# Expert stage: TensorE reads a slot's weight address behind the gate/up block of the slot ahead

## The chip, the cores and the metric

One core of a Trainium2 chip. The metric is the device time of the kernel in microseconds (us). The engines of the core are TensorE (PE; its weight loads are PEld), VectorE (DVE), ScalarE (ACT), GpSimd (POOL) and SyncE (SP).
## The reference

Cross-attention on 64 x 64 tokens of width 256, then a mixture of eight experts with two experts for each token:

```python
x = x + xattn(layernorm(x), ctx_2048, ...)          # 16 heads; not touched by the change
h = layernorm(x)
probs = softmax(h @ gate_w.T); topw, sel = top_k(probs, 2)
combine = topw / sum(topw), put at the columns sel   # (T, E), T = 4096, E = 8
g, u = split(h @ w1[e].T)                            # w1: (8, 2*176, 256)
expert_out[e] = (silu(g) * u) @ w2[e].T              # w2: (8, 256, 176)
x = x + sum over e of combine[:, e] * expert_out[e]
```

## The kernel before

The first part, up to about 358 us, does the attention, the routing and the sorting: each token's normalised row is written twice to a table in HBM (sorted_rows), grouped by expert. A short plan then gives 72 slots of 128 rows each, and for every slot the first row and the offset of its expert's weights. All experts' weights lie in the on-chip memory (we_h and we_l, a high and a low part). The offsets are 72 whole numbers in slot_w, a view of the tile square.

The expert stage, 372 to 536 us, runs over the 72 slots in a software pipeline. In turn i, TensorE does four blocks, each for another slot:

- tr_hs(i), L1321: two transposes of the slot's rows (hs). They wait for the DMA that loads the rows.
- gate_up(i-1), L1328: six matmuls of 352 columns (L1110, L1111, L1112, twice each). They wait for h2_l_ready, which VectorE sets when it has made the low part of the transposed rows (L1068), behind ScalarE's high part (L703).
- tr_act(i-2), L1339 and L1340: two transposes of silu(g) * u. They wait for act_ready (ScalarE L709, VectorE L1075).
- down(i-3), L1342: six matmuls of 256 columns, with the same three lines. They wait for au_l_ready (ScalarE L714, VectorE L1081).

Behind them ScalarE copies the result (L721) and GpSimd scatters it to HBM (L528). A last stage of some 40 us loads these results, adds the two of each token and stores the output.

gate_up and down address the weights by a register. weights_of(m), L1324 to L1326, fills it: a load of one word of slot_w into a register of TensorE's sequencer (TENSOR_LOAD), with register work around it (FUSED_REGOPS in the trace, ISA in the program) and a check of the bounds. gate_up(i-1) and, two turns later, down(i-3) use the same register, kept in found[r].

The turns come in passes of RING = 12. The first pass is written out, five passes are a loop on each engine (Fori, L1397), and three last turns are written out again. found lives in one pass: in the turns r = 0 and r = 1 the down block's slot belongs to the pass before, and its address is read anew, just ahead of down. In the views tiles are named by the memory that they share: late is hs, xt_h and xt_l are the transposed rows, probs is the activation, at_h and at_l the transposed activation, and bank is the PSUM memory.

Of the kernel before, what the change touches and what calls it, by code (L numbers as in the profile page):

```python
# [36 lines left out]
NSLOT = 72  # L37
RING = 12
# [47 lines left out]
def build_in(nc, stack, x, ctx_t, w_proj, w_out, w_exp, w_gate, bias, norm_q, norm_k, out,  # L86
# [1018 lines left out]
    def _(pe):  # L1105
# [3 lines left out]
        def three(dst, a_h, a_l, b_h, b_l, start, stop):  # L1109
            pe.matmul(dst, a_h, b_h, start=start, stop=False)  # L1110
            pe.matmul(dst, a_h, b_l, start=False, stop=False)  # L1111
            return pe.matmul(dst, a_l, b_h, start=False, stop=stop)  # L1112
# [204 lines left out]
        def tr_hs(m, p, j, r):  # L1317

            pe.wait_ge(hs_loaded[r], (j + 1) * 16)
            for c in range(KC):  # L1320
                ins = pe.transpose(bank[:, p, c * P:(c + 1) * P], hs[:, r, c * P:(c + 1) * P], ident[:, :])  # L1321
            ins.then_inc(F["h2_transposed"], 1)

        def weights_of(m):  # L1324

            return pe.value_load(slot_w[0:1, bass.ds(m, 1)], min_val=0, max_val=(NE - 1) * EW)  # L1326

        def gate_up(m, p, w):  # L1328

            pe.wait_ge(F["h2_l_ready"], m + 1)  # L1330
            for c in range(KC):
                w_h, w_l = (t[:, c * 2 * FI:][:, bass.ds(w, 2 * FI)] for t in (we_h, we_l))
                ins = three(bank[:, 2 + p, 0:2 * FI], hst_h[:, p, c, :], hst_l[:, p, c, :], w_h, w_l, c == 0, c == KC - 1)
            ins.then_inc(F["gate_up"], 1)

        def tr_act(m, p):

            pe.wait_ge(F["act_ready"], m + 1)
            pe.transpose(bank[:, 4 + p, 0:P], act_u[:, p, 0:P], ident[:, :])  # L1339
            pe.transpose(bank[:, 4 + p, P:2 * P], act_u[:, p, P:2 * P], ident[:, :]).then_inc(F["act_transposed"], 1)  # L1340

        def down(m, p, w, last):  # L1342
            pe.wait_ge(F["au_l_ready"], m + 1)

            if last:
                pe.wait_ge(F["y_ready"], m - 1)
            for n in range(2):
                w_h, w_l = (t[:, 2 * KC * FI + n * D:][:, bass.ds(w, D)] for t in (we_h, we_l))
                ins = three(bank[:, 6 + p, 0:D], au_h[:, p, n, :], au_l[:, p, n, :], w_h, w_l, n == 0, n == 1)
            ins.then_inc(F["y_done"], 1)  # L1350
# [7 lines left out]
        found = {}  # L1358

        def turn2(j, r, static):  # L1360
            i = j * RING + r
            gates = not static or 0 <= i - 1 < NSLOT
            if gates:
                found[r] = weights_of(i - 1)
            if not static or i < NSLOT:
                tr_hs(i, r % 2, j, r)
            if gates:
                gate_up(i - 1, (r - 1) % 2, found[r])
            if not static or 0 <= i - 2 < NSLOT:
                tr_act(i - 2, r % 2)  # L1370
            if not static or 0 <= i - 3 < NSLOT:
                down(i - 3, (r - 3) % 2, found[r - 2] if r >= 2 else weights_of(i - 3), not gates)

        slots(pe, turn2)

# [72 lines left out]
```

## Time and profile before

| what | value |
|---|---|
| three timed runs | 577.34, 579.50, 579.65 us; median 579.5 |
| profiled execution | 580.65 us, span 578.9 us |
| TensorE busy, whole span | 468.8 us (81%) |
| expert stage (TensorE) | about 372 to 536 us |
| one turn in mid-pass | 2.12 us |

The span runs from the first to the last instruction of the program; the time of an execution is a little longer. A matmul in the timeline is shown with its start and its length; the lengths of neighbours overlap, since the array takes the next one in before the last one is out. The distance between starts is what a matmul costs in a row of them. "issue" as the cause of an idle time means that the profile shows nothing that the engine waited for: its sequencer had not got there yet.

### The profile page before, as it was taken

The numbers are of one execution on the slowest core, as the hardware profiler recorded it, in microseconds if no ns is written. First come the engines' busy times: TensorE is split into PE (matmuls) and PEld (weight loads), VectorE is DVE, ScalarE is ACT, GpSimd is POOL, SyncE is SP. The second block draws the span as 40 slices with busy tenths as digits, with TensorE's granted clock in tenths as the row PEclk, the third lists the DMA queues.
The fourth block names the chain that finished last, engine by engine and source line by source line (L and its number), as shares of the span: only waits on it lengthen the run. The fifth ranks groups of instructions, "written<-read, shape, count | busy, mean of one in ns | idle before, by whom it ended". The sixth has DMA issues, their size and how long they took to land.

```text
span 578.9 us, 16175 instructions
## 1 busy us (share of the span) xinstructions
PE 468.8 (81%) x4192; PEld 420.6 (73%) x4193; DVE 404.6 (70%) x1215; ACT 315.3 (54%) x934; POOL 303.7 (52%) x531
## 2 busy tenths in 40 slices
PE   2879999889989998999999972299999999999000
PEld 1668888778877787878888762299999999999000
DVE  7457988888898898988899966054545454455265
ACT  4466767666766766676667531155555555555000
POOL 6544466766676676767676646234444443444100
PEclk9789999999999999999999986599999999999755
DMA  7132342222222122222212112524434343331599
GB/s 221 49 105 58 105 138 65 78 69 68 75 66 68 61 74 65 70 73 68 75 62 76 48 47 92 146 77 125 117 106 127 102 119 109 113 105 55 168 384 318
DMA packets 55919, 60.02 MB, mean 104 GB/s; under 512 B 7871, under 2 KB 51530, under 8 KB 55882
## 3 DMA queue, kind: packets, MB, share of 16 engines
q1 hardware_dynamic: 44426, 38.00, 22.9%
q0 software_dynamic: 6528, 16.86, 8.4%
q10 hardware_dynamic: 4928, 4.72, 2.4%
q8 instruction: 17, 0.28, 0.2%
q14 instruction: 20, 0.16, 0.1%
HBM read 32.86 MB, written 23.27 MB: 97 GB/s over the span
## 4 chain that ended last, share of the span: by engine, by line
PE 52%; issue 14%; POOL 12%; ACT 6%; SPq 5%; DVE 5%; DMA 3%; POOLq 1%; ACTq 0%; another core or an unknown queue 0%; DVEq 0%
PE bank L1110 11%; PE bank L1112 10%; PE bank L1111 10%; PE bank L1170 6%; SPq L383 4%; PE bank L1321 3%; ACT probs L622 2%; POOL sorted_rows L458 2%; POOL r_qk L416 2%; PE bank L1158 2%; PE bank L1118 2%; DMA we_l<-expert_out 2%; PE bank L1143 2%; PE bank L1339 1%; PE bank L1340 1%
## 5 line engine op out<-in xcount | busy, mean ns | idle before, releaser
L528 POOL DMA_INDIRECT expert_out<-probs,late x72 | 69.8, 969 | 102.7 <-ACT probs L721 91.9
L458 POOL DMA_INDIRECT sorted_rows<-row,place_i x64 | 66.0, 1031 | 42.2 <-issue 22.0
L565 ACT CAST qp_h<-bank 32x256 f16<-32x256 f32 x128 | 46.5, 363 | 54.3 <-PE bank L1143 51.9
L1068 DVE TENSOR_TENSOR xt_l<-bank,xt_h 128x256 fp32r<-128x256 f32 x72 | 30.6, 425 | 55.2 <-ACT xt_h L703 55.0
L842 DVE TENSOR_TENSOR qp_l<-bank,qp_h 32x256 f16<-32x256 f32 x128 | 53.2, 416 | 10.8 <-ACT qp_h L565 7.7
L1170 PE MATMUL bank<-v_bd,probs 128*64 128x34 f32 x1024 | 59.1, 225 | 0.0
L1170 PEld LDWEIGHTS bank<-v_bd,probs 128*64 128x64 f32 x1024 | 55.5, 138 | 3.5 <-issue 0.2
L1110 PE MATMUL bank<-we_h,xt_h 128*128 x144 | 53.4, 371 | 0.1
L1075 DVE SCALAR_TENSOR_TENSOR probs<-xn,late,bank 128x176 f32<-128x176 f32 x72 | 28.6, 398 | 34.7 <-PE bank L1340 18.3
L1110 PE MATMUL bank<-we_h,at_h 128*128 x144 | 46.6, 324 | 1.1 <-issue 0.5
L1112 PE MATMUL bank<-we_h,xt_l 128*128 x144 | 47.2, 327 | 0.0
L1111 PE MATMUL bank<-we_l,xt_h 128*128 x144 | 47.1, 327 | 0.0
L709 ACT ACTIVATE xn<-bank 128x176 f32<-128x176 f32 x72 | 22.9, 319 | 40.2 <-PE bank L1112 35.0
L1321 PE MATMUL bank<-ident,late 128*128 128x128 f32 x144 | 29.1, 284 | 18.2 <-DMA late<-sorted_rows 16.1
L721 ACT COPY probs<-bank 128x256 f32<-128x256 f32 x72 | 26.9, 373 | 28.7 <-PE bank L1112 22.0
L416 POOL TENSOR_TENSOR rstd<-veps,half_neg 128x1 f32<-128x1 f32 x64 | 36.1, 564 | 9.5 <-POOL veps L414 3.9
L1112 PE MATMUL bank<-we_h,at_l 128*128 x144 | 40.7, 283 | 0.0
L1111 PE MATMUL bank<-we_l,at_h 128*128 x144 | 40.3, 280 | 0.0
L847 DVE TENSOR_REDUCE row_max<-bank 128x16 f32<-128x1024 f32 x32 | 38.8, 1214 | 0.0
L1220 PE MATMUL bank<-qp_h,late 128*128 128x256 f16 x128 | 35.5, 277 | 3.1 <-ACT neg_max_t L587 1.8
L703 ACT CAST xt_h<-bank 128x256 fp32r<-128x256 f32 x72 | 27.2, 377 | 19.2 <-PE bank L1321 17.8
L1224 PE MATMUL bank<-neg_max_t,head_of 128*128 128x128 bf16 x256 | 35.5, 221 | 0.0
(194 smaller groups left out, 1590.3 us busy)
## 6 DMA issues: line engine op xcount, KB each, us to landing
late<-sorted_rows SPq DMA_DIRECT2D x72, 129.0 KB
we_f<-w_exp SPq DMA_DIRECT2D x32, 152.0 KB
v_bd<-v_sb SPq DMA_DIRECT2D x128, 34.0 KB, 1.9
ctx_in<-ctx_t SPq DMA_DIRECT2D x32, 128.0 KB, 2.2
we_h<-expert_out SPq DMA_DIRECT2D x16, 256.0 KB, 6.0
we_l<-expert_out SPq DMA_DIRECT2D x16, 256.0 KB, 9.2
x<-x SPq DMA_DIRECT2D x3, 1024.0 KB, 5.9
out<-we_h ACTq DMA_DIRECT2D x8, 256.0 KB, 5.9
```

The source lines that it names most:

```text
L416: pool.tensor_tensor(out_, tmp, half_neg[:, 0:tmp.shape[1]], ALU.pow).then_inc(done_, 1)
L458: pool.indirect_dma_start(sorted_rows, bass.IndirectOffsetOnAxis(ap=place_i[:, t.slot // 2, k, t.par:t.par + 1], axis=0), row[:, k, t.slot ...
L528: pool.indirect_dma_start(expert_out, bass.IndirectOffsetOnAxis(ap=hs[:, r, D:D + 1].bitcast(U32), axis=0), y_sb[:, r % YRING, :], None, b ...
L565: act.copy(q_part(qp_h, t, g), q_bank(g)).then_inc(S["q_h_ready"], 1)
L842: dve.tensor_tensor(q_part(qp_l, t, g), q_bank(g), q_part(qp_h, t, g), ALU.subtract).then_inc(S["q_l_ready"], 1)
L847: dve.tensor_reduce(row_max[:, t.par, :], score_bank.rearrange("p (h k) -> p h k", h=NH), AX.X, ALU.max).then_inc(S["max_found"], 1)
L1110: pe.matmul(dst, a_h, b_h, start=start, stop=False)
L1111: pe.matmul(dst, a_h, b_l, start=False, stop=False)
L1112: return pe.matmul(dst, a_l, b_h, start=False, stop=stop)
L1170: ins = pe.matmul(av_bank[b * L:(b + 1) * L, g * 2 * VW:(g + 1) * 2 * VW], probs[:, t.par, at:at + L], v_bd[:, t.par, b, :, g * VW:(g + 1) ...
L1220: pe.matmul(dst, k_h, q_h, start=True, stop=False)
L1321: ins = pe.transpose(bank[:, p, c * P:(c + 1) * P], hs[:, r, c * P:(c + 1) * P], ident[:, :])
```

## The change

In turn2 of TensorE the read of the address that gate_up(i) will use, which stood at the head of turn i+1, stands in turn i, between gate_up(i-1) and tr_act(i-2). Only the turn r = 0 of each pass still reads its own address at its head, since found isn't carried from one pass to the next, and the turn r = 11 reads none. The reads for down in the turns r = 0 and r = 1 are as they were. The number of reads stays, 84.

```diff
         def turn2(j, r, static):
             i = j * RING + r
             gates = not static or 0 <= i - 1 < NSLOT
-            if gates:
+            if gates and r == 0:
                 found[r] = weights_of(i - 1)
             if not static or i < NSLOT:
                 tr_hs(i, r % 2, j, r)
             if gates:
                 gate_up(i - 1, (r - 1) % 2, found[r])
+            if r < RING - 1 and (not static or 0 <= i < NSLOT):
+                found[r + 1] = weights_of(i)
             if not static or 0 <= i - 2 < NSLOT:
                 tr_act(i - 2, r % 2)
             if not static or 0 <= i - 3 < NSLOT:
                 down(i - 3, (r - 3) % 2, found[r - 2] if r >= 2 else weights_of(i - 3), not gates)
```

In TensorE's program of the loop, before the change, at the seam of the turns r = 2 and r = 3 (the last matmuls of down, then the read, then the transposes of the next slot):

```order
L1111 MATMUL bank<-we_l,at_h 128x256
L1112 MATMUL bank<-we_h,at_l 128x256
L1326 ISA
L1326 TENSOR_LOAD square
L1326 ISA x2
L1321 MATMUL bank<-ident,late 128x128 [waits hs_loaded3]
L1321 MATMUL bank<-ident,late 128x128
L1330 REGISTER_ALU
L1110 ISA [waits h2_l_ready]
```

After the change, in the turn r = 2, behind the last matmuls of gate/up:

```order
L1111 MATMUL bank<-we_l,xt_h 128x352
L1112 MATMUL bank<-we_h,xt_l 128x352
L1326 ISA
L1326 TENSOR_LOAD square
L1326 ISA x2
L1339 MATMUL bank<-ident,probs 128x128 [waits act_ready]
L1340 MATMUL bank<-ident,probs 128x128
L1110 ISA [waits au_l_ready]
```

The read (ISA, TENSOR_LOAD, ISA x2) has moved from behind down to ahead of tr_act, and down is followed by the transposes at once. The waits for h2_l_ready and au_l_ready stand on the first register instruction of gate/up and of down; those for the loaded rows and for act_ready stand on matmuls.

The second place is the first turn of a pass in the loop, r = 0, from the end of gate/up to the beginning of down. Before:

```order
L1112 MATMUL bank<-we_h,xt_l 128x352
L1338 REGISTER_ALU
L1339 MATMUL bank<-ident,probs 128x128 [waits act_ready]
L1340 MATMUL bank<-ident,probs 128x128
L1326 ISA
L1326 TENSOR_LOAD square
L1326 ISA x2
L1343 REGISTER_ALU
L1110 ISA [waits au_l_ready]
L1110 MATMUL bank<-we_h,at_h 128x256
```

After:

```order
L1112 MATMUL bank<-we_h,xt_l 128x352
L1326 ISA
L1326 TENSOR_LOAD square
L1326 ISA x2
L1338 REGISTER_ALU
L1339 MATMUL bank<-ident,probs 128x128 [waits act_ready]
L1340 MATMUL bank<-ident,probs 128x128
L1326 ISA
L1326 TENSOR_LOAD square
L1326 ISA x2
L1343 REGISTER_ALU
L1110 ISA [waits au_l_ready]
```

Ahead of down in r = 0 there are two reads now, one ahead of tr_act and one behind it. At the end of the same turn, before (the second half of down, then the turn r = 1):

```order
L1111 REGISTER_ALU
L1111 MATMUL bank<-we_l,at_h 128x256
L1112 MATMUL bank<-we_h,at_l 128x256
L1326 ISA
L1326 TENSOR_LOAD square
L1326 ISA x2
L1321 MATMUL bank<-ident,late 128x128 [waits hs_loaded1]
L1321 MATMUL bank<-ident,late 128x128
L1330 REGISTER_ALU
L1110 ISA [waits h2_l_ready]
```

After:

```order
L1111 REGISTER_ALU
L1111 MATMUL bank<-we_l,at_h 128x256
L1112 MATMUL bank<-we_h,at_l 128x256
L1321 MATMUL bank<-ident,late 128x128 [waits hs_loaded1]
L1321 MATMUL bank<-ident,late 128x128
L1330 REGISTER_ALU
L1110 ISA [waits h2_l_ready]
```

The read between down and the transposes of r = 1 is gone.

## Rows read from the trace of the kernel before

**Rows 1.** The page of the whole execution: TensorE's busy time; the chain's shares.
```profile
PE 468.8 (81%) x4192; PEld 420.6 (73%) x4193; DVE 404.6 (70%) x1215; ACT 315.3 (54%) x934; POOL 303.7 (52%) x531
...
PE 52%; issue 14%; POOL 12%; ACT 6%; SPq 5%; DVE 5%; DMA 3%; POOLq 1%; ACTq 0%; another core or an unknown queue 0%; DVEq 0%
```

**Rows 2.** Stretches: from:to, length, busy us of PE, PEld, DVE, ACT, POOL, PEclk.
```profile
420.00:440.00 20.00, 19.51 (x143) 18.56 (x142) 10.33 (x27) 10.95 (x36) 8.71 (x9) 1.00 0.39 116
```

**Rows 3.** Timeline of TensorE in mid-pass: start, length, what, [idle before it].
```profile
412.88 0.38 PE L1321 MATMUL bank<-ident,late 128*128 128x128 f32 x2
...
414.07 0.27 PE L1339 MATMUL bank<-ident,probs 128*128 128x128 f32 x1
...
414.20 0.36 PE L1110 MATMUL bank<-we_h,at_h 128*128 x1
...
415.00 0.38 PE L1321 MATMUL bank<-ident,late 128*128 128x128 f32 x2
```

**Rows 4.** Line L1326 on TensorE's sequencer (PEldq), whole execution: ns min/median/max.
```profile
L1326 PEldq FUSED_REGOPS  x149: 46/151/168, 372.3 to 534.3; - x149
L1326 PEldq TENSOR_LOAD <-square x84: 296/303/491, 371.7 to 534.0; - x84
```

**Rows 5.** Single lines in 412.5 to 415.05 us: ns, first to last start.
```profile
L1110 PEldq FUSED_REGOPS  x2: 46/46/46, 413.4 to 413.6; - x2
...
L1326 PEldq FUSED_REGOPS  x2: 46/98/151, 413.9 to 414.3; - x2
...
L1110 PEldq FUSED_REGOPS  x2: 42/44/46, 414.7 to 415.0; - x2
...
L1081 DVE TENSOR_TENSOR at_l<-bank,at_h x1: 425/425/425, 412.9 to 412.9; 128x256 fp32r<-128x256 f32 x1
...
L1068 DVE TENSOR_TENSOR xt_l<-bank,xt_h x1: 424/424/424, 413.8 to 413.8; 128x256 fp32r<-128x256 f32 x1
```

**Rows 6.** Waits in 385 to 535 us: us in total, times, longest.
```profile
PEld bank L1321 <- issue: 4.2, 11, 0.4
...
PEld bank L1110 <- issue: 2.7, 7, 0.7
```

**Rows 7.** Timeline of TensorE at the top of the second loop pass.
```profile
423.50 0.43 PE L1321 MATMUL bank<-ident,late 128*128 128x128 f32 x2
...
425.26 0.38 PE L1110 MATMUL bank<-we_h,at_h 128*128 x1
...
426.40 0.44 PE L1321 MATMUL bank<-ident,late 128*128 128x128 f32 x2 [0.16 <-issue]
...
427.88 0.38 PE L1110 MATMUL bank<-we_h,at_h 128*128 x1
...
429.04 0.44 PE L1321 MATMUL bank<-ident,late 128*128 128x128 f32 x2 [0.18 <-issue]
...
431.26 0.38 PE L1321 MATMUL bank<-ident,late 128*128 128x128 f32 x2
```

**Rows 8.** Timeline of TensorE at the top of the first loop pass.
```profile
396.99 0.38 PE L1321 MATMUL bank<-ident,late 128*128 128x128 f32 x2
...
404.40 0.38 PE L1321 MATMUL bank<-ident,late 128*128 128x128 f32 x2
```

**Rows 9.** TensorE's sequencer at the top of the second loop pass, single lines.
```profile
L1397 PEldq COMPARE_BRANCH  x1: 221/221/221, 422.3 to 422.3; - x1
...
L1326 PEldq TENSOR_LOAD <-square x1: 443/443/443, 424.3 to 424.3; - x1
...
L1326 PEldq FUSED_REGOPS  x2: 46/98/151, 427.0 to 427.5; - x2
...
L1110 PEldq FUSED_REGOPS  x2: 46/46/46, 427.8 to 428.0; - x2
```

**Rows 10.** Timeline of TensorE soon after the start of the stage.
```profile
377.75 0.38 PE L1321 MATMUL bank<-ident,late 128*128 128x128 f32 x2
...
382.15 0.38 PE L1321 MATMUL bank<-ident,late 128*128 128x128 f32 x2
```

## The prediction

> **What bounds the kernel now.** I read the page first. TensorE is busy for 468.8 us, 81% of the span, and holds 52% of the chain that ended last [rows 1]. The table by stretches shows the stage that the change touches: between 420 and 440 us TensorE is busy for 19.51 of 20.00 us at the full clock (2.4 GHz), VectorE, ScalarE and GpSimd for about half of it or less [rows 2]. So the expert stage, some 372 to 536 us, is a TensorE stage. What is left to win in it is the rest that TensorE idles, and what a change can lose is new idle time there.
>
> Next, the timeline of TensorE in the middle of a loop pass. The transposes of the incoming slot (L1321) start at 412.88 and 415.00, one turn = 2.12 us, and nothing in between carries an idle time [rows 3]. In such a turn the array loses nothing to the read of the weight address. The read itself is work of TensorE's sequencer, the part that hands instructions to the array. The rows of L1326 show it: a TENSOR_LOAD of 303 ns, 84 times, and register work of 151 ns behind it [rows 4]. The 84 are 72 slots and 12 repeats, since the turns r = 0 and r = 1 of a pass read a second address, that of slot i-3, for their down block.
>
> **How far ahead the sequencer is.** In the middle of a pass it starts the down block's register work at 413.4, the down matmul it prepares runs at 414.20: 0.8 us ahead. It could not be earlier: the first register instruction of that block carries the wait on au_l_ready, and VectorE's at_l (0.425 us from 412.9 on) ends at 413.3 [rows 5, 3]. Then comes the read from 413.9 on and the gate/up block of the next turn at 414.7 [rows 5]; the array starts that turn at 415.00. The blocks are: down 0.5 (413.4 to 413.9), a read 0.75 (427.0 to 427.8, nothing between, less rounding), and 0.6 for gate/up with the register work of the transposes (from L1321 at 426.40 to the read at 427.0) [rows 5, 7, 9]. One turn of sequencer work is about 1.85 us out of 2.12, and 0.3 us is spent waiting. The Trainium skill ("Advanced Engine Details and Errata", Sequencer Loop and Engine Queue Depths) has it that an engine instruction is queued and waits in the queue, 64 deep on TensorE, while the sequencer goes on; by that rule alone the sequencer would be many turns ahead and no read could ever cost anything. The row disagrees for this kernel: the waits for h2_l_ready and au_l_ready stand on register instructions, and the lead is 0.8 us.
>
> **Where TensorE idles.** The weight-load side of TensorE waits 4.2 us before L1321 and 2.7 us before L1110 in 385 to 535 us, both put down to "issue", time with nothing to wait for that the profile knows [rows 6]. They lie almost all at one place, the top of the loop. In the loop pass that begins with the turn at 423.50 the turns last 2.90, 2.64 and 2.22 us (423.50, 426.40, 429.04, 431.26), 1.40 us more than three times 2.12 [rows 7]. Four of the five loop passes do this within 0.03 us; the first, entered without a taken branch, loses 1.05 us (three turns in 396.99 to 404.40, 7.41 us) [rows 8]. The cause is in the sequencer: a branch of 0.22 us [rows 9], and then two reads in each of two turns, so that a turn needs 1.85 + 0.75 = 2.6 us of sequencer against 2.12 of array. The sequencer is the bound from 424 to 429 us, and only there.
>
> **What the change does.** It moves 66 reads (r = 1 to 11 of six passes) from ahead of the transposes L1321 to behind the gate/up block of the turn before: back across down and tr_act. The read of r = 0 stays, so the turn r = 0 now has three reads in it instead of two, r = 1 two as before, r = 11 none. Count and kind of instructions stay the same (84 reads, no DMA, no new wait), and in the last three turns the order is as before. SP, ScalarE, VectorE and GpSimd get no edit.
>
> Middle of a pass: the read now lies between gate/up and tr_act. What it would hold back is tr_act (L1339) and down. The gate/up register work can start at 414.2, when h2_l is ready (VectorE's xt_l, 0.424 us from 413.8 on) [rows 5], takes 0.5 of its 0.6, the read 0.75: the sequencer reaches tr_act at about 415.45; the array wants it at 414.07 + 2.12 = 416.19 [rows 3]. Cover 0.7 us. If this cover were gone, the price would be the overshoot times some 60 turns. I take 0.
>
> Top of the loop, pass at 423.50, with the durations of [rows 7, 9]. The sequencer ends the gate/up block of r = 0 at 424.1, two register instructions ahead of the load at 424.3. Now it reads the next address (the load there took 443 ns, so 0.9): 425.0. tr_act goes at 425.05, where the array wants it at 423.50 + 1.19 = 424.7. Then the read for slot i-3, 0.75, ahead of down: one more read than before stands there, so down goes to the array at 425.26 + 0.75 = 426.01. It holds the array for 0.80 us [rows 3], 0.83 after a stall as I take it, so the next transposes start at 426.84 instead of 426.40, **+0.44**. For the sequencer there is no read between down and L1321 any more: down's register work, 425.9 + 0.5, brings it to 426.4, the very time of before. Gate/up to 427.0, read to 427.75, read to 428.5: down of r = 1 at 428.6 instead of 427.88, 0.83 us of array, next transposes at 429.43 instead of 429.04, **+0.40**. From there the turn takes 2.12 instead of 2.22: 431.55 against 431.26, **+0.29** is what stays. In words: the number of reads done before each L1321 is unchanged, but the last late point is now ahead of down (0.83 of array behind it) and not behind it (0.5 of sequencer ahead of it), and the array no longer runs its down block under a read. Four loop passes: 4 x 0.29 = +1.16.
>
> First loop pass, by the same steps without the branch and with a load of 0.30: gate/up ends at 397.2, down at 399.0, transposes at 399.8, two reads to 401.4, down, transposes at 402.33, then 404.45 against 404.40 [rows 8]: +0.06. Start of the stage: the two turns from 377.75 to 382.15 last 4.40 instead of 4.24 [rows 10]; a read stands there behind the first wait for au_l, and moved ahead of that wait it is covered: -0.15.
>
> Sum: 1.16 + 0.06 - 0.15 = +1.07 us. Behind the stage everything (last scatter, loads of the results, sum, store) hangs on TensorE's last block, so it ends 1.1 later. The profiled execution took 580.65 us for a span of 578.9, and would be 581.7; it lay 1.15 above the median of the three timed runs (579.5), so as a median I predict **580.6 us**, +0.2%.
>
> The cost of a read is bounded from below by its load alone, 0.30 us, and from above by 0.95 us (the 491 ns maximum plus the 0.45 around it) [rows 4]. With 0.3 a two-read turn needs 1.7 us, under 2.12, and only the start of the stage is left: -0.15. With 0.95 the difference of 0.83 and 0.5 stays, and tr_act is held 0.2 more in each of five passages: about +2. I take 0.75, the spacing in the rows. The Trainium skill ("DMA: Bandwidth & Descriptors", Latency and other measured facts) gives a floor of about 600 ns for a tensor_load; the trace has 303 ns. With 600 a turn would need 2.15 us of sequencer, just over the array's 2.12, and the steady turns before would show idle time, which they do not.
>
> **The rivals.**
> - *Slower, 12%: a passage loses a whole read.* Now two reads stand back to back ahead of down, after a taken branch. If the array's late start at down is not won back, because tr_hs, gate/up and the wait for au_l of the next turn all shift with it, each passage loses the 0.75 by which down is late: 5 x 0.75 = 3.8 us, 583.3. For it: tr_act itself is held 0.3 us, and the chain tr_act, ScalarE, VectorE, down starts from it. Against it: that chain has 0.8 us of slack [rows 5]. It decides when the slack of a turn falls under 0.75.
> - *Slower in every turn, 3%*: the cover of 0.7 us in the middle of a pass fails, 60 turns x 0.1 us or more, 586 and over. It takes a read of more than 1.4 us.
> - *No change, 20%: nothing to see.* The sequencer is late by the same sum of reads either way and the array ends the passage at the same time, 579.5. The Trainium skill's rule of the 64 deep queue ("Advanced Engine Details and Errata", Engine Queue Depths) would give this result too. Against it: the step of 0.83 against 0.5 above.
> - *Faster, 7%: the stalls go.* The idle time before L1321 (4.2 us on the weight-load side [rows 6]) vanishes and down finds its addresses in time. That needs the sequencer to be early at the top of the loop, which the 2.6 us of a two-read turn speak against. 579.5 - 4.2 = 575.3. It decides if r = 0 and r = 1 could be fed from addresses read earlier; they are not, they keep three and two reads.
>
> My forecast has 58%, of which 2% beyond +0.5%.
>
> **The numbers.** A measurement of this kernel tells 0.5% (2.9 us) from no change: the three runs lie 2.3 us apart. The range 577.9 to 583.6 holds the forecast, the case of no change and nearly all of the first slower one with the scatter of runs; faster and slower in every turn lie outside. Faster by over 0.5%: 0.07. Slower by over 0.5%: about two thirds of the first slower rival, the second and the 2%, 0.13. Same: 0.80.
>
> **What would show it.** In the middle of a pass: turns of 2.12 us as now, L1326 starting while gate/up runs. At the top: idle time before L1321 gone, a larger one before the down block's L1110 in r = 0 and r = 1 and a small one before L1339, turns of about 3.3, 2.6 and 2.1 us instead of 2.90, 2.64 and 2.22. It would be wrong if turns of 2.12 grow anywhere else, if the three turns still add to 7.76, or if a load slows down in its new place.

## The result

The changed kernel takes 580.13 us (median of 19 runs, 577.25 to 582.76) against 578.27 (19 runs, 575.92 to 580.21) before. The ratio is 1.0027, with a 95% interval of 1.0015 to 1.0040. That is 1.6 us slower (the two medians lie 1.9 apart), a small loss, but one that 19 runs tell from none. The likeliest case of the prediction was 580.6 us, +1.07 us.

The page of the profiled execution. Its span is 2.3 us shorter than that of before, although the kernel is slower: single executions scatter by more than the change is worth, and in this one the expert stage began 2.7 us earlier.

```profile
span 576.6 us, 16175 instructions
...
PE 465.4 (81%) x4192; PEld 418.1 (73%) x4193; DVE 404.1 (70%) x1215; ACT 314.5 (55%) x934; POOL 303.4 (53%) x531
```

The waits of the same stretch as in [rows 6], 385 to 535 us:

```profile
PEld bank L1110 <- issue: 6.9, 11, 0.8
...
PEld bank L1339 <- issue: 1.9, 4, 0.5
```

L1321 is gone from the list (4.2 us on the weight-load side before), L1110 has gone from 2.7 to 6.9 us, and 1.9 us before L1339 is new. The stalls have moved from ahead of the transposes to ahead of the down block and of tr_act, and they have grown. In the middle of a pass nothing has changed. TensorE's timeline there, to be held against [rows 3]:

```profile
412.59 0.38 PE L1321 MATMUL bank<-ident,late 128*128 128x128 f32 x2
...
413.78 0.27 PE L1339 MATMUL bank<-ident,probs 128*128 128x128 f32 x1
...
414.71 0.38 PE L1321 MATMUL bank<-ident,late 128*128 128x128 f32 x2
...
415.90 0.27 PE L1339 MATMUL bank<-ident,probs 128*128 128x128 f32 x1
```

Turns of 2.12 us. The reads of that stretch (412 to 417.2 us; ns min/median/max, first and last start):

```profile
L1326 PEldq TENSOR_LOAD <-square x3: 297/303/306, 412.4 to 416.7; - x3
L1326 PEldq SEQ_ASSERT  x2: 18/18/18, 413.0 to 415.1; - x2
```

The check that ends a read starts at 413.0 and the tr_act behind it runs at 413.78; one turn later 415.1 and 415.90. The cover is 0.8 us, 0.7 was forecast.

The top of the second loop pass, which answers to [rows 7]:

```profile
421.12 0.43 PE L1321 MATMUL bank<-ident,late 128*128 128x128 f32 x2
...
422.76 0.33 PE L1339 MATMUL bank<-ident,probs 128*128 128x128 f32 x1 [0.24 <-issue]
...
423.72 0.38 PE L1110 MATMUL bank<-we_h,at_h 128*128 x1 [0.53 <-issue]
...
424.53 0.38 PE L1321 MATMUL bank<-ident,late 128*128 128x128 f32 x2
...
426.33 0.38 PE L1110 MATMUL bank<-we_h,at_h 128*128 x1 [0.24 <-issue]
...
427.14 0.38 PE L1321 MATMUL bank<-ident,late 128*128 128x128 f32 x2
...
429.26 0.38 PE L1321 MATMUL bank<-ident,late 128*128 128x128 f32 x2
```

The three turns last 3.41, 2.61 and 2.12 us, 8.14 in sum against 7.76. At the first loop pass ([rows 8]) they take 7.75 against 7.41:

```profile
394.24 0.38 PE L1321 MATMUL bank<-ident,late 128*128 128x128 f32 x2
...
397.11 0.38 PE L1321 MATMUL bank<-ident,late 128*128 128x128 f32 x2
...
399.82 0.38 PE L1321 MATMUL bank<-ident,late 128*128 128x128 f32 x2
...
401.99 0.38 PE L1321 MATMUL bank<-ident,late 128*128 128x128 f32 x2
```

Over the whole stage, from the first transposes to those of the last slot, the profiled execution of before took 158.15 us (371.73 to 529.88) and that of after 158.73 (369.06 to 527.78), 0.58 longer. The parts are these:

- The tops of the five loop passes: +1.75 (three turns each: 38.45 in sum before, 40.20 after).
- The start of the stage: the fourth and fifth turn -0.15 (2.12 and 2.12 instead of 2.22 and 2.17), the third +0.07 (2.51 instead of 2.44). The third turn scatters from 1.91 to 2.61 over the thirteen traces.
- The execution of before had one turn of 3.14 us in mid-pass and one of 2.21 behind it, 1.11 too long together, at a pause of ScalarE (last section): -1.11.
- All other turns: +0.02.

Without the pause the change costs 1.69 us in these two traces, and 1.60 in the turns that the prediction spoke of. The timed runs say 1.6.

### The profile page after: what moved, and what is told of

Same layout as the page of the kernel before. It is cut to its first block, busy times and chain, and to the rows that moved or that the text cites. A ratio compares the mean times of both kernels' runs of the same rounds, so it can differ in the third digit from the quotient of the medians.

```text
span 576.6 us, 16175 instructions
## 1 busy us (share of the span) xinstructions
PE 465.4 (81%) x4192; PEld 418.1 (73%) x4193; DVE 404.1 (70%) x1215; ACT 314.5 (55%) x934; POOL 303.4 (53%) x531
## 4 chain that ended last, share of the span: by engine, by line
PE 50%; issue 15%; POOL 14%; ACT 6%; SPq 5%; DVE 4%; DMA 3%; POOLq 1%; ACTq 0%; DVEq 0%
PE bank L1110 11%; PE bank L1111 10%; PE bank L1112 10%; PE bank L1170 5%; SPq L383 4%; PE bank L1321 3%; POOL sorted_rows L458 3%; ACT probs L622 3%; POOL r_qk L416 2%; PE bank L1158 2%; DMA we_l<-expert_out 2%; POOL rstd L416 2%; PE bank L1339 2%; POOL row L445 1%; PE bank L1118 1%
## 5 line engine op out<-in xcount | busy, mean ns | idle before, releaser
L1110 PE MATMUL bank<-we_h,xt_h 128*128 x144 | 53.3, 370 | 0.1
L1110 PE MATMUL bank<-we_h,at_h 128*128 x144 | 46.7, 324 | 4.3 <-issue 3.9
L709 ACT ACTIVATE xn<-bank 128x176 f32<-128x176 f32 x72 | 22.9, 318 | 37.6 <-PE bank L1112 37.6
L1321 PE MATMUL bank<-ident,late 128*128 128x128 f32 x144 | 28.4, 280 | 16.4 <-DMA late<-sorted_rows 16.2
```

## The experiments

In each of them I read the turns, the distances between the first transposes of neighbouring slots, from the timeline. In most kernels they repeat from pass to pass within some hundredths of a us (where a slow load is at work, within 0.2), while the timed runs tell 1 us only just. Each kernel has one trace. Unless said otherwise the excerpt is the second loop pass.

**Where the loss sits: the middle of the passes alone.** In the changed kernel:

```diff
-            if gates and r == 0:
+            if gates and r <= 2:
                 found[r] = weights_of(i - 1)
...
-            if r < RING - 1 and (not static or 0 <= i < NSLOT):
+            if 2 <= r < RING - 1 and (not static or 0 <= i < NSLOT):
                 found[r + 1] = weights_of(i)
```

> Only the reads for the turns r = 3 to 11 of each pass are moved behind gate/up; r = 1 and r = 2 read at their head as in the kernel before. Theory (the loss is at the top of the loop, where reads now stand ahead of down): the three turns after a loop top stay at 2.90, 2.64 and 2.22 us, the middle of the pass at 2.12, and the time is that of before within 0.3 us (the start of the stage may give 0.15). Rival (the moved reads cost something in every turn, or the program's new layout does): the loss of 1.6 us is here, and turns in mid-pass are longer than 2.12.

```profile
420.19 0.43 PE L1321 MATMUL bank<-ident,late 128*128 128x128 f32 x2
...
423.11 0.43 PE L1321 MATMUL bank<-ident,late 128*128 128x128 f32 x2 [0.17 <-issue]
...
425.76 0.43 PE L1321 MATMUL bank<-ident,late 128*128 128x128 f32 x2 [0.18 <-issue]
...
428.07 0.38 PE L1321 MATMUL bank<-ident,late 128*128 128x128 f32 x2
```

Measured: ratio to before 1.0015 (0.9997 to 1.0033). Turns of 2.92, 2.64, 2.32 and then 2.12. The sums of the three turns are 7.57 and 7.86 to 7.88, 0.12 a passage more than before, 0.6 us in all, less the 0.15 of the start. From r = 3 to r = 10 no turn is over 2.13. So the rival is out for mid-pass. But my "within 0.3" missed something: this edit makes a new two-read turn. r = 2 reads its own address at its head and the next one behind gate/up, and its length rises from 2.22 to between 2.32 and 2.38.

**The top of the loop alone.**

```diff
-            if gates and r == 0:
+            if gates and r not in (1, 2):
                 found[r] = weights_of(i - 1)
...
-            if r < RING - 1 and (not static or 0 <= i < NSLOT):
+            if r < 2 and (not static or 0 <= i < NSLOT):
                 found[r + 1] = weights_of(i)
```

> Only the reads for r = 1 and r = 2 are moved, all others stand as in the kernel before. Theory: the whole effect of the change is here: turns of 3.4, 2.6 and 2.12 us at each loop top, 0.35 us more a passage, 1.5 to 1.8 us in all. Rival (cost in mid-pass or of the layout): time of before, turns 2.90, 2.64, 2.22.

```profile
425.51 0.43 PE L1321 MATMUL bank<-ident,late 128*128 128x128 f32 x2
...
428.92 0.38 PE L1321 MATMUL bank<-ident,late 128*128 128x128 f32 x2
...
431.55 0.38 PE L1321 MATMUL bank<-ident,late 128*128 128x128 f32 x2
...
433.67 0.38 PE L1321 MATMUL bank<-ident,late 128*128 128x128 f32 x2
```

Measured: ratio 1.0033 (1.0017 to 1.0050), turns of 3.41, 2.63 and 2.12, the five sums 1.79 us over those of before (1.75 in the changed kernel). The whole loss of the change is made by the two moved reads of each pass.

**Which of the two reads.** Each alone, from the kernel before. This is the read for r = 1, moved into r = 0; for the read for r = 2, moved into r = 1, the two conditions have `r != 2` and `r == 1`.

```diff
-            if gates:
+            if gates and r != 1:
                 found[r] = weights_of(i - 1)
...
+            if r == 0 and (not static or 0 <= i < NSLOT):
+                found[r + 1] = weights_of(i)
```

> Only the read for the turn r = 1 is moved, into r = 0 behind gate/up; all others stand as in the kernel before. Theory (the passage ends at the last point at which the sequencer is late, plus the array work behind it): down of r = 0 is late as in the changed kernel, but the last late point is the transposes of r = 2 again, behind the same five reads as in the kernel before. Turns of 3.35 to 3.4, about 2.2 and 2.2 us, their sum 7.76 as before (within 0.1), time of before. Rival (two reads back to back ahead of down in r = 0 are what costs): sum 8.1, +1.6 us.

```profile
424.94 0.43 PE L1321 MATMUL bank<-ident,late 128*128 128x128 f32 x2
...
428.35 0.38 PE L1321 MATMUL bank<-ident,late 128*128 128x128 f32 x2
...
430.52 0.43 PE L1321 MATMUL bank<-ident,late 128*128 128x128 f32 x2
...
432.74 0.38 PE L1321 MATMUL bank<-ident,late 128*128 128x128 f32 x2
```

> Only the read for the turn r = 2 is moved, into r = 1 behind gate/up; all others stand as in the kernel before. Theory: down of r = 1 is now the last late point with a down block of the array behind it. Turns of 2.90, 3.0 and 2.12 us, their sum 8.05 to 8.15 against 7.76: the whole loss of the change, +1.5 to +1.8 us, from this one read. Rival (the pair in r = 0 is what costs): sum 7.76.

```profile
423.30 0.43 PE L1321 MATMUL bank<-ident,late 128*128 128x128 f32 x2
...
426.24 0.43 PE L1321 MATMUL bank<-ident,late 128*128 128x128 f32 x2 [0.19 <-issue]
...
429.31 0.38 PE L1321 MATMUL bank<-ident,late 128*128 128x128 f32 x2
...
431.43 0.38 PE L1321 MATMUL bank<-ident,late 128*128 128x128 f32 x2
```

Measured: with the read for r = 1 alone the turns are 3.40, 2.18 and 2.22, and the sum is 7.80 here and 7.74 to 7.75 in the later passes: that of before, though two reads stand ahead of down in r = 0 and down is as late as in the changed kernel. With the read for r = 2 alone they are 2.94, 3.07 and 2.12, sum 8.13, as in the changed kernel. The timed ratios are 1.0028 (1.0005 to 1.0051) and 1.0047 (1.0029 to 1.0065). The second is clear. The first is higher than the turns explain, since no passage of that trace is slower than before by more than 0.04 us; what the rest of it is stays open. So the split between the two reads is shown by the turns; the timed runs alone would not show it, since the two ratios add up to 0.75%, more than the 0.33% of both reads together.

This is the sharpest of the tests. A late point is one at which the array waits for the sequencer. One read costs nothing in the turns, since a later late point follows it (the transposes of r = 2) that comes no later than before. The other, the same instructions one turn later, costs all of it, since it sits ahead of the last late point.

**The second reads moved to the head of the turn.** In the kernel before:

```diff
+            if r < 2 and (not static or 0 <= i - 3 < NSLOT):
+                old = weights_of(i - 3)
             if gates:
                 found[r] = weights_of(i - 1)
...
-                down(i - 3, (r - 3) % 2, found[r - 2] if r >= 2 else weights_of(i - 3), not gates)
+                down(i - 3, (r - 3) % 2, found[r - 2] if r >= 2 else old, not gates)
```

> The kernel before, with the second reads of r = 0 and r = 1 (slot i-3) moved from ahead of down to the head of the turn, so that two reads stand back to back there, ahead of the transposes. Theory (what counts is the work that the array still has behind the last late point; the number of reads ahead of the transposes of r = 2 is the same, so the passage ends as before): r = 11 takes 2.9, r = 0 2.6, r = 1 and r = 2 2.12 us; the four together 9.75 us against 9.90 before, time within 0.8 us of before and rather below it. Rival (two reads back to back cost a whole read of 0.75 us a passage): the four turns take 10.6 us, and the kernel is 3.8 us slower.

```profile
422.10 0.38 PE L1321 MATMUL bank<-ident,late 128*128 128x128 f32 x2
...
424.96 0.43 PE L1321 MATMUL bank<-ident,late 128*128 128x128 f32 x2 [0.58 <-issue]
...
427.97 0.44 PE L1321 MATMUL bank<-ident,late 128*128 128x128 f32 x2 [0.67 <-issue]
...
430.20 0.38 PE L1321 MATMUL bank<-ident,late 128*128 128x128 f32 x2
...
432.32 0.38 PE L1321 MATMUL bank<-ident,late 128*128 128x128 f32 x2
```

Measured: ratio 1.0021 (1.0004 to 1.0038); the four turns (r = 11 to r = 2) are 2.86, 3.01, 2.23 and 2.12, 10.22 against 9.90 before, and 1.25 us more over the five passages. Neither sum was right. I had put the last late point before the transposes of r = 2; in the trace it is before those of r = 1 (0.67 us of idle time there, none before r = 2), with a whole turn of array work behind it. The load ahead of it took 542 ns, which the expectation did not have. Where that load took only 432 ns, in the third loop pass, the four turns still sum to 10.08. The rival's 10.6 is out: a pair of reads does not cost a whole read by being a pair. The rule of the last late point can be read into this result, but only afterwards; this run does not test it.

**The read made shorter.** In both orders, the check of the bounds taken away:

```diff
         def weights_of(m):
-            return pe.value_load(slot_w[0:1, bass.ds(m, 1)], min_val=0, max_val=(NE - 1) * EW)
+            reg = pe.alloc_register()
+            pe.reg_load(reg, slot_w[0:1, bass.ds(m, 1)])
+            return pe.snap(reg, donate=True, min_val=0, max_val=(NE - 1) * EW)
```

> The order of before, each read without the check of its bounds (the register work of 151 ns and the check of 18 ns go, what is computed stays). A read is then 0.46 us of sequencer instead of 0.75, a two-read turn 2.0 instead of 2.6, under the 2.12 of the array. Theory: the loss at the loop tops is gone or nearly, three turns of 6.4 to 6.6 us, 572.5 to 573.5 us (ratio 0.989 to 0.991), like the kernel that carries the addresses. Rival (the stall is the branch and what follows it in fetching code): more than half of the 6.7 us stays, ratio over 0.994.

> The same short read in the order of the changed kernel. Theory: the order matters only while a two-read turn is longer than 2.12 us; now it makes no difference, within 0.5 us of the kernel with the short read in the order of before, sums of the three turns 6.4 to 6.6. Rival (the order itself costs, whatever the read's length): 1.6 us more than that kernel.

The read's rows in the first of the two, whole execution (the line is L1327 there):

```profile
L1327 PEldq TENSOR_LOAD <-square x84: 297/305/488, 371.5 to 526.4; - x84
L1327 PEldq FUSED_REGOPS  x65: 46/46/51, 396.3 to 521.1; - x65
```

The second, at the top of the second loop pass:

```profile
419.80 0.38 PE L1321 MATMUL bank<-ident,late 128*128 128x128 f32 x2
...
422.12 0.38 PE L1321 MATMUL bank<-ident,late 128*128 128x128 f32 x2
...
424.25 0.38 PE L1321 MATMUL bank<-ident,late 128*128 128x128 f32 x2
```

Measured: in the order of before 0.9889 (0.9868 to 0.9911), every turn at the loop tops 2.12 us, all three-turn sums 6.36. In the new order 0.9909 (0.9881 to 0.9938); one turn of each passage is 2.32 to 2.38, 1.1 us over the five. The branch alone does not make the stall of the loop tops: with the same branch and shorter reads it is gone, and in the kernel before the first loop pass loses 1.05 of the 1.40 us without a taken branch ahead of it. And my "within 0.5 us" for the new order was wrong by the turns (the two timed intervals overlap). It puts three reads into r = 0, and even short ones are then late by 0.2 us; in the first loop pass it is r = 1 that is late (2.38), where one load took 547 ns.

**The addresses carried over the loop's back edge.** In the changed kernel, with three registers:

```diff
         found = {}
+        keep = [pe.alloc_register(f"keep{n}") for n in range(3)]
+
+        def kept(n):
+            return pe.snap(keep[n], min_val=0, max_val=(NE - 1) * EW)
...
             if gates and r == 0:
-                found[r] = weights_of(i - 1)
+                found[r] = kept(2)
...
-            if r < RING - 1 and (not static or 0 <= i < NSLOT):
+            if not static or 0 <= i < NSLOT:
                 found[r + 1] = weights_of(i)
+            if r == RING - 1:
+                for n in range(3):
+                    pe.reg_mov(keep[n], found[r - 1 + n])
...
-                down(i - 3, (r - 3) % 2, found[r - 2] if r >= 2 else weights_of(i - 3), not gates)
+                down(i - 3, (r - 3) % 2, found[r - 2] if r >= 2 else kept(r), not gates)
```

> The changed kernel, but three registers carry the addresses over the loop's back edge: r = 11 reads the address for the next pass too, and neither r = 0 at its head nor r = 0 and r = 1 ahead of down read anything. 72 reads instead of 84, one a turn. Theory (the sequencer is the bound only where a turn holds more than one read: 1.85 us with one, 2.6 with two): all turns take 2.12 us, a branch of 0.22 us is within the lead of 0.8, and the loss of the five passages, 1.05 + 4 x 1.42 = 6.7 us in the kernel before, is gone: 571.5 us against 578.3, ratio 0.988. Rival (the branch, or fetching the code behind it, makes most of the stall): more than half of the 6.7 us stays.

```profile
422.07 0.38 PE L1321 MATMUL bank<-ident,late 128*128 128x128 f32 x2
...
424.20 0.38 PE L1321 MATMUL bank<-ident,late 128*128 128x128 f32 x2
...
426.32 0.38 PE L1321 MATMUL bank<-ident,late 128*128 128x128 f32 x2
```

Measured: 572.39 us, ratio 0.9895 (0.9865 to 0.9924). Every turn at every loop top is 2.12 us; the stage takes 150.0 us instead of the 158.1 of before, in which the pause of ScalarE had 1.1. This version beats both kernels, and its reads keep their check. Most of the 6.7 us that were expected are there: the loop tops are 6.65 us shorter.

**TensorE's turns written out.**

```diff
-                down(i - 3, (r - 3) % 2, found[r - 2] if r >= 2 else weights_of(i - 3), not gates)
-
-        slots(pe, turn2)
+                down(i - 3, (r - 3) % 2, found[(i - 2) % 12], not gates)
+
+        for i in range(NSLOT + 3):
+            turn2(i // RING, i % RING, True)
```

> The order of before, but TensorE's 75 turns written out, without a loop: constant addresses, 72 reads, one a turn at its head, no branch; its program grows from 1,411 to some 2,600 rows. Theory: as in the kernel that carries the addresses, every turn 2.12 us, 6.7 us less, ratio 0.988 to 0.990. Rival (a longer straight program stalls TensorE where new code is fetched): turns above 2.12 at places that have nothing to do with reads, ratio over 0.992.

The loads from 396 us on:

```profile
L1326 PEldq TENSOR_LOAD <-square x60: 295/390/504, 397.7 to 523.8; - x60
```

Measured: 571.55 us, ratio 0.9832 (0.9793 to 0.9870). All turns are 2.11 to 2.13 us from r = 5 of the first pass on, but for one of 3.01 and one of 2.17 behind it, at a pause of ScalarE; without them the stage takes 150.0 us like that of the kernel with carried addresses. The loads are slower here than in the loop, 390 ns in the median against 303 [rows 4], and with one of them a turn the array loses nothing. By the traces the two kernels are equal; the ratios, from different chips, differ by more than that, and why they do wasn't tried.

**How much the middle of a pass can hide.** The changed kernel with more reads behind the moved one:

```diff
                 found[r + 1] = weights_of(i)
+                if r in (6,):
+                    weights_of(i)
```

> The changed kernel with one more read in the turn r = 6 of every pass, behind the moved one; its value isn't used. Theory (in mid-pass the sequencer reaches tr_act some 0.6 to 0.7 us before the array does, and a turn of it has 0.3 us to spare): the 0.75 us are covered all but 0.0 to 0.2 us, once a pass, 0 to 1.2 us in all. Rival (a read behind gate/up is not covered, it costs its length): 0.75 us a pass, 4.5 us.

> The changed kernel with one more read in each of the turns r = 5 to 8. Theory: four turns of 2.6 us of sequencer against 2.12 of array, 1.9 us too much, of which the lead takes 0.6 once: 1.2 to 1.9 us a pass, 7 to 11 us in all, and turns of 2.6 us among r = 5 to 9 as at the loop top. Rival (the sequencer runs many turns ahead, as a queue of 64 would let it): no turn over 2.2 us. Second rival (each read costs its length): 3.0 us a pass, 18 us.

With one extra read the time is 580.16 us (one run; seven of the kernel before on that chip have the median 580.72, the changed kernel was not timed there) and every turn r = 3 to 11 stays at 2.11 to 2.13, but for one of 2.92 in the whole trace. With four of them, in turns r = 5 to 8, for which the condition reads `r in (5, 6, 7, 8)`, the second loop pass goes on like this (437.37 is the start of r = 5, the first turn with an extra read):

```profile
437.37 0.38 PE L1321 MATMUL bank<-ident,late 128*128 128x128 f32 x2
...
439.55 0.38 PE L1321 MATMUL bank<-ident,late 128*128 128x128 f32 x2
...
442.08 0.38 PE L1321 MATMUL bank<-ident,late 128*128 128x128 f32 x2
...
444.85 0.38 PE L1321 MATMUL bank<-ident,late 128*128 128x128 f32 x2
...
447.46 0.38 PE L1321 MATMUL bank<-ident,late 128*128 128x128 f32 x2
...
449.66 0.38 PE L1321 MATMUL bank<-ident,late 128*128 128x128 f32 x2
```

The loads from r = 7 to r = 9 (442.3 to 448.0 us):

```profile
L1326 PEldq TENSOR_LOAD <-square x5: 300/430/629, 442.3 to 447.7; - x5
```

Measured: 589.31 us (one run; before 580.72). The first turn is 2.18, then 2.53, 2.77, 2.61 and 2.20: 1.7 us over five turns of 2.12, and about 9 us more in mid-pass in all. A sum for the 1.7, worked out afterwards and an estimate: an extra read has no register work ahead of its load and takes 0.64 us instead of 0.75, so a turn with it needs 1.85 + 0.64 = 2.49 us of sequencer, 0.37 over the array's 2.12, four times 1.5. Loads of 538, 430 and 629 ns instead of 300 add 0.7, and the lead of 0.6 comes off: 1.6. The loads that slow down are a part of this cost that the expectation did not have. One extra read is covered whole and four in a row are not; a lead of many turns is out by that, and so is the price of a whole read each.

## Why the prediction was right

- **TensorE's sequencer bounds the loop tops.** Shown: taking two reads out of the passage (carried addresses) or making them shorter takes the stall away, with the branch still there.
- **Middle of a pass, cost 0.** Shown by the traces of the change and of the version with mid-pass reads alone (0.8 us of cover against 0.7 forecast), and by the extra reads: one is hidden, four are not.
- **Top of the loop, +0.44, +0.40, then +0.29.** The instants were forecast as distances from the transposes of r = 0 at 423.50. After stands 421.12 for it. tr_act: 1.55 forecast, 1.64 measured; down of r = 0: 2.51 and 2.60; transposes of r = 1: 3.34 and 3.41; down of r = 1: 5.10 and 5.21; transposes of r = 2: 5.93 and 6.02; of r = 3: 8.05 and 8.14. Each step is 0.07 to 0.11 late, and one row can account for all of it, the load of the moved read:

```profile
L1326 PEldq TENSOR_LOAD <-square x1: 561/561/561, 421.7 to 421.7; - x1
```

  It took 561 ns where I had carried over the 443 of [rows 9]; in the other three passes 487, 523 and 517, and their three turns sum to 8.06, 8.13 and 8.10 against the 8.05 forecast. The four passes with a taken branch cost 1.40 us instead of 1.16. "A load slows down in its new place" stood in the prediction as a sign of being wrong. It came: the mechanism held, and the slower load can account for the 0.24 that this term was short. Why the load slows down stays open.
- **The last late point.** That the loss is not a read's length, but the difference between the 0.83 us of array work in down and the 0.5 of sequencer work for it, is borne out by the two reads moved singly: in the turns only the one ahead of the last late point costs.
- **First loop pass, +0.06: mis-sized.** Measured +0.35. The mechanism was that of the others, and two reads in it took longer than the 0.75 and 0.30 that I put in. One read behind gate/up of r = 1 took 0.92 us from its start to the next instruction with a load of 302 ns, and the load in r = 2 was long:

```profile
L1326 PEldq TENSOR_LOAD <-square x1: 566/566/566, 400.1 to 400.1; - x1
```

  It holds tr_act of r = 2, and the turn becomes 2.17. This term, 0.29 short, and the 0.24 of the four others make the step from +1.07 to the measured +1.60.
- **Start of the stage, -0.15.** Measured: 2.124 and 2.120 instead of 2.224 and 2.170, -0.15. The version with the mid-pass reads alone has it too, those without them don't.
- **Behind the stage, nothing.** From the last slot's transposes to the end of the span it is 49.0 us before and 48.8 after.
- **The time, 580.6 against 580.13, is in part luck.** The prediction started from the median of three runs, 579.5, and 19 runs give 578.27. So the start was 1.2 us too high and the step at least 0.5 too small, and the two cancel. What can be held to the prediction's credit is the direction, the place and the turns, not the half microsecond between the two times.
- **The rivals.** "A passage loses a whole read", 3.8 us: out, the passage loses 0.35. "No change": out, though by 0.27% only; the range had to hold it. "Slower in every turn": out. "Faster, the stalls go": they did go before L1321, and came back before L1110.

## What to carry to other kernels

An engine's sequencer has a time of its own for each turn of a loop, and reading an address into a register is its dearest item here (0.75 us with the check, against 2.12 us a turn). As long as a turn of this kernel held one such read, its place made no difference in mid-pass. Where turns at the loop's edge held two or three, moving them moved the stall, and the loss was set by the array work behind the last point where the sequencer was late: a read ahead of down cost 0.35 us a passage more than the same read behind it, where it ran while the array did the down block. What helps is fewer or shorter loads at the edge: carrying the values in registers over the back edge took 1.05% off this kernel.

## What the runs showed of the hardware

- Some register loads take longer than the 300 ns of most, and many of these recur at the same place in every pass. In the kernel before, the loads that start 1.91 to 1.94 us after the taken branch take 443 to 476 ns; in the changed one those that start at 1.80 to 1.82 take 487 to 561. But the time since the branch does not explain it. In the changed order with short reads, loads that start at 2.10 to 2.13 us take 298 to 320 ns; with the mid-pass reads alone, loads at 9.2 us take 508 to 549 in each of the four passes; and with the turns written out, without a branch, the median of the loads is 390 ns and the longest behind the start of the stage 504. The kernel with carried addresses has no load over 313 ns but the first. What holds a load was not found; the fetching of instructions wasn't tried.
- The check of a read's bounds costs nearly as much of the sequencer as the load: without it a read takes 0.46 to 0.52 us at the second loop top instead of 0.75.
- ScalarE paused once for 2.0 to 2.2 us before L709, at 487 to 496 us, in six of the thirteen traces, the one of before among them, and for 1.4 us in a seventh, the one with the turns written out. It was always in the turn r = 8 of the fourth loop pass, and made that turn 0.8 to 1.2 us longer, half or more of what the change is worth. The other six traces don't have it. With one trace of each kernel, whether it goes with the execution or with the edit isn't shown.
